# Selective scan of layer 1: the gated input written over u in SBUF, where the state's scan reads it, with four u buffers

## The chip, the cores and the metric

The kernel runs on one core of one Trainium2 chip. The metric is the device time of one launch in microseconds (us). An instruction of one of the engines TensorE (PE in the rows), VectorE (DVE), ScalarE (ACT), GpSimd (POOL) and SyncE (SP, which only issues DMAs here) runs in the order of its engine's program, and the engines wait for each other through semaphores.

## The reference

Two layers over 32 images of 96 channels by 56 x 56 pixels, all in float32. Layer 0 is a depthwise 7x7 convolution, a layer norm over channels, a two-layer MLP and a residual. Layer 1, where the change is, is a depthwise 5x5 convolution with SiLU and then a selective scan over the L = 3136 pixels of an image, with N = 4 states for each channel:

```python
xs = silu(conv5x5(x) + conv_b)                      # (B, D, L)
x_dbl = einsum('kd,bdl->bkl', x_proj_w, xs)         # dts, Bs, Cs
delta = softplus(einsum('dr,brl->bdl', dt_w, dts) + dt_b)
log_dA = maximum(delta[:, :, None] * A, LOG_EPS)
P = exp(cumsum(log_dA, axis=-1))
dB_u = delta[:, :, None] * Bs[:, None] * xs[:, :, None]
hs = P * cumsum(dB_u / maximum(P, EPS), axis=-1)
y = einsum('bdnl,bnl->bdl', hs, Cs) + xs * Ds
```

The kernel computes hs as a recurrence. With d_a = exp(log_dA), q is the running product of d_a that starts at 1/EPS, so that q = P/EPS; the input of the state is multiplied by min(q, 1), which stands for the maximum(P, EPS) of the reference; and h is the recurrence h = d_a * h + min(q, 1) * u.

## The kernel before

The two layers run one after the other. Layer 0 ends near 1,850 us of the profiled execution and layer 1's recurrence runs from 1,988 us to its end.

Layer 1 works on groups of 4 images, so there are 8 groups. 128 partitions hold 32 channels of 4 images, so a group has TILES = 3 such tiles. The 3136 pixels are cut into BANDS = 7 bands of BT = 448. For each band and tile there are N = 4 states, so a band has 12 steps and a group S = 84 steps; the kernel has 672. Every engine's program for a group is a Python loop over the steps s, written out, and its order is the order of the calls; there is no scheduler.

In one step:

- ScalarE writes d_a (L1211 and L1217), five steps ahead, into one of seven buffers.
- GpSimd writes u = dxs * B (`times_b`, L1029), U_AHEAD steps ahead. It multiplies a finished h by C in place (`times_c`, L1042), and, but for the last band, first copies the last column of h (h_last, L1039, a 128x1 addition with zeros). In 3 of 12 steps it also makes dxs = delta * xs (`times_x`, L1017), between the two.
- VectorE runs, for step s: `keep_q` (L1113, a copy of the last column of q, not in the last band), `gate` (L1121), in 3 of 12 steps `sum_delta` (L1095), then `scan_q` of step s + 1 (L1105) and `scan_h` of step s (L1132).
- TensorE adds the four h*C of a tile into ps_y (L1354), and computes the convolution of the next group of images beside it (L1299, L1306, and, in bursts, L1319).

The two q buffers ps_q are PSUM banks. `scan_q` reads d_a from SBUF and a broadcast zero column no_q from PSUM. `gate` reads q and u and writes over q in the PSUM bank. `scan_h` reads d_a from SBUF and the gated values from PSUM, and writes h to SBUF. `sum_delta` reads one operand from PSUM and one from SBUF. GpSimd reads and writes SBUF alone.

GpSimd's program for step s is `times_c` of s - 1, then `times_x` where there is one, then `times_b` of s + U_AHEAD. `times_b` waits until the buffer that it writes is free, which is told by the semaphore gated.

Of the kernel before, what the change touches and what calls it, by code (L numbers as in the profile page):

```python
# [39 lines left out]
BT = BLKS * TOK  # L40
BANDS = L // BT
# [35 lines left out]
SLABS = 3  # L77
AHEAD = 5
ZSTEPS = 3
U_SLOTS = 3  # L80
U_AHEAD = U_SLOTS
H_SLOTS = 6
Y_LAG = 2
Z_SLOTS = 2
DA_SLOTS = 7
# [635 lines left out]
def layer1(nc, groups, x1, t2, consts, out):  # L721
# [4 lines left out]
    with ExitStack() as ctx:  # L726
        def sb(name, shape, dt=F32):
            return ctx.enter_context(nc.sbuf_tensor(name, shape, dt))

        def pb(name):  # L730
            return ctx.enter_context(nc.psum_tensor(name, [128, BANK], F32))

        def sem(name):
            return ctx.enter_context(nc.semaphore(name))
# [22 lines left out]
        d_a = [sb(f"d_a{i}", [128, BT]) for i in range(DA_SLOTS)]  # L757
        b_rows = [sb(f"b_rows{i}", [128, BT]) for i in range(N)]
        u = [sb(f"u{i}", [128, BT]) for i in range(U_SLOTS)]
        c_rows = [sb(f"c_rows{i}", [128, BT]) for i in range(N)]  # L760
        h = [sb(f"h{i}", [128, BT]) for i in range(H_SLOTS)]
# [6 lines left out]
        ps_q = [pb(f"ps_q{i}") for i in range(2)]  # L768
# [25 lines left out]
        gated = sem("gated")  # L794
        h_done = sem("h_done")
        hc_done = sem("hc_done")
        q_kept = sem("q_kept")
# [10 lines left out]
        S = BANDS * STEPS  # L808
        RUNS = BANDS * TILES
        KEPT = (BANDS - 1) * STEPS  # L810
# [73 lines left out]
        def next_band(g, b):  # L884
            return (g, b + 1) if b + 1 < BANDS else (g + 1, 0)
# [114 lines left out]
        @block.gpsimd  # L1000
        def _(pool):
            nc.gpsimd.memset(zeros[:, :], 0.0).then_inc(prepared, 1)
            nc.gpsimd.memset(q_first[:, :], float(np.float32(1) / np.float32(EPS))).then_inc(prepared, 1)
            nc.gpsimd.memset(log_eps[:, 0:1], -LOG_EPS).then_inc(prepared, 1)
            for k in range(Y_SLOTS):
                pool.sem_inc(y_stored[k], 16)
            pool.sem_inc(y_kept, 1)
            pool.sem_inc(h_done, 1)
            pool.sem_inc(gated, 1)
            pool.sem_inc(y_added, H_SLOTS)  # L1010
            pool.wait_ge(prepared, PREPARED)

            def times_x(f, b, t, first=False):
                pool.wait_ge(delta_ready, f * RUNS + b * TILES + t + 1)
                if not first:
                    pool.wait_ge(u_done, (f * BANDS + b - 1) * STEPS + (t + 1) * N)  # L1016
                nc.gpsimd.tensor_tensor(dxs[:, t, :], delta[:, t, :], xs[:, t, b * BT:(b + 1) * BT],  # L1017
                                        ALU.mult).then_inc(dxs_ready, 1)

            def times_b(g, s, first=False):  # L1020

                b, t, n = s // STEPS, s % STEPS // N, s % N
                if t == 0:
                    pool.wait_ge(b_in[n], (g * BANDS + b + 1) * 16)
                if n == 0:
                    pool.wait_ge(dxs_ready, g * RUNS + s // N + 1)
                if not first:
                    pool.wait_ge(gated, g * S + s - U_SLOTS + 2)
                nc.gpsimd.tensor_tensor(u[s % U_SLOTS][:, :], dxs[:, t, :], b_rows[n][:, :],  # L1029
                                        ALU.mult).then_inc(u_done, 1)  # L1030

            def times_c(g, s):

                b, t, n = s // STEPS, s % STEPS // N, s % N
                if t == 0:
                    pool.wait_ge(c_in[n], (g * BANDS + b + 1) * 16)
                pool.wait_ge(h_done, g * S + s + 2)  # L1037
                if b + 1 < BANDS:
                    nc.gpsimd.tensor_tensor(h_last[:, s % STEPS:s % STEPS + 1], h[s % H_SLOTS][:, BT - 1:BT],  # L1039
                                            zeros[:, 0:1], ALU.add).then_inc(h_kept, 1)  # L1040
                    pool.wait_ge(h_kept, g * KEPT + s + 1)
                nc.gpsimd.tensor_tensor(h[s % H_SLOTS][:, :], h[s % H_SLOTS][:, :], c_rows[n][:, :],  # L1042
                                        ALU.mult).then_inc(hc_done, 1)

            def group(g, more, first=False):
                for s in range(S):
                    b, j = s // STEPS, s % STEPS
                    f, fb = next_band(g, b)
                    prepare = more or b + 1 < BANDS

                    if s > 0:
                        times_c(g, s - 1)
                    if prepare and j in DXS_AT:
                        times_x(f, fb, DXS_AT.index(j))
                    if j == DXS_NOW:
                        times_x(g, b, TILES - 1, b == 0 and first)
                    if prepare and j + U_AHEAD == STEPS - N:

                        pool.wait_ge(xd_stored, (f * BANDS + fb + 1) * 16)
                    if s + U_AHEAD < S:  # L1060
                        times_b(g, s + U_AHEAD)
                    elif more:
                        times_b(g + 1, s + U_AHEAD - S)
                times_c(g, S - 1)


            for t in range(TILES - 1):
                times_x(0, 0, t, True)
            for s in range(U_AHEAD):
                times_b(0, s, True)  # L1070
            group(0, True, True)
            with pool.Fori(1, last) as g:
                group(g, True)
            group(last, False)

        @block.vector
        def _(dve):
# [20 lines left out]
            def scan_q(g, s):  # L1098
                b, j = s // STEPS, s % STEPS
                dve.wait_ge(d_a_ready, g * S + s + 1)  # L1100
                dve.wait_ge(h_done, g * S + max(s, 1))
                if s > 1:
                    dve.wait_ge(q_kept, g * KEPT + min(s - 1, KEPT))  # L1103
                first = q_first[:, 0:1] if b == 0 else q_last[:, j:j + 1]
                nc.vector.tensor_tensor_scan(ps_q[s % 2][:, 0:BT], d_a[s % DA_SLOTS][:, :],  # L1105
                                             no_q.broadcast_to([128, BT]), first,
                                             ALU.mult, ALU.add).then_inc(q_done, 1)
# [7 lines left out]
            def gate(g, s):  # L1115
                b = s // STEPS
                dve.wait_ge(q_done, g * S + s + 1)
                if b + 1 < BANDS:
                    dve.wait_ge(q_kept, g * KEPT + s + 1)
                dve.wait_ge(u_done, g * S + s + 1)  # L1120
                nc.vector.scalar_tensor_tensor(ps_q[s % 2][:, 0:BT], ps_q[s % 2][:, 0:BT], 1.0, u[s % U_SLOTS][:, :],  # L1121
                                               ALU.min, ALU.mult).then_inc(gated, 1)

            def scan_h(g, s):
                b, j = s // STEPS, s % STEPS
                dve.wait_ge(gated, g * S + s + 2)
                dve.wait_ge(y_added, g * S + s + 1)
                first = zeros[:, 0:1]
                if b > 0:
                    dve.wait_ge(h_kept, g * KEPT + s - STEPS + 1)  # L1130
                    first = h_last[:, j:j + 1]
                nc.vector.tensor_tensor_scan(h[s % H_SLOTS][:, :], d_a[s % DA_SLOTS][:, :], ps_q[s % 2][:, 0:BT], first,  # L1132
                                             ALU.mult, ALU.add).then_inc(h_done, 1)

            def group(g, more):
                scan_q(g, 0)
                for s in range(S):
                    b, j = s // STEPS, s % STEPS
                    f, fb = next_band(g, b)
                    keep_q(g, s)  # L1140
                    gate(g, s)
                    if (more or b + 1 < BANDS) and j in SUM_AT:
                        sum_delta(f, fb, SUM_AT.index(j))
                    if s + 1 < S:
                        scan_q(g, s + 1)
                    scan_h(g, s)
# [327 lines left out]
```

## Time and profile before

| | |
|---|---|
| median of 3 runs | 4056.53 us (4040.93 to 4058.47) |
| the profiled execution, its own time | 4053.06 us |
| its span, first to last instruction | 4051.3 us |
| a middle group of layer 1, first scan_h to first scan_h of the next | 259.58 us |
| the last group, first to last scan_h | 242.84 us |
| granted TensorE clock, mean | 0.93 |

A span is shorter than the time of its execution by what lies before the first and behind the last instruction, here 1.8 us. Busy times of different engines overlap. An idle time in a row is that of the engine ahead of the instructions of the group, with what ended it behind an arrow.

### The profile page before, as it was taken

The numbers are of one execution on the slowest core, as the hardware profiler recorded it, in microseconds if no ns is written. First come the engines' busy times: TensorE is split into PE (matmuls) and PEld (weight loads), VectorE is DVE, ScalarE is ACT, GpSimd is POOL, SyncE is SP. The second block draws the span as 40 slices with busy tenths as digits, with TensorE's granted clock in tenths as the row PEclk, the third lists the DMA queues.
The fourth block names the chain that finished last, engine by engine and source line by source line (L and its number), as shares of the span: only waits on it lengthen the run. The fifth ranks groups of instructions, "written<-read, shape, count | busy, mean of one in ns | idle before, by whom it ended". The sixth has DMA issues, their size and how long they took to land. (4 is left out here: it accounts for less than half of the span.)

```text
span 4051.3 us, 72657 instructions
## 1 busy us (share of the span) xinstructions
PE 3669.9 (91%) x22358; PEld 2643.2 (65%) x22358; DVE 3170.4 (78%) x4640; ACT 2564.9 (63%) x4292; POOL 2309.4 (57%) x2448
## 2 busy tenths in 40 slices
PE   6999999999999999997899898998989989899776
PEld 6778787979787787867566564664646646556322
DVE  3676858585766768580399899998998989989999
ACT  1453718172645537274688788787877878778764
POOL 0232404141322324140398897988988889888988
PEclk9999999999999999997799898898988989989887
DMA  7546473746465464427565555564546646455321
GB/s 229 166 139 197 103 245 96 248 101 218 120 188 160 133 206 105 169 75 161 137 172 152 146 167 131 168 170 127 169 125 172 181 115 181 133 159 161 94 74 61
DMA packets 383776, 613.07 MB, mean 151 GB/s; under 512 B 199967, under 2 KB 324152, under 8 KB 383048
## 3 DMA queue, kind: packets, MB, share of 16 engines
q1 hardware_dynamic: 383336, 607.74, 52.7%
q8 instruction: 211, 3.46, 0.4%
q14 instruction: 229, 1.88, 0.1%
HBM read 527.35 MB, written 80.28 MB: 150 GB/s over the span
## 5 line engine op out<-in xcount | busy, mean ns | idle before, releaser
L523 ACT ACTIVATE act_h<-ps_up,b 128x448 f32<-128x448 f32 x672 | 408.9, 635 | 781.7 <-PE ps_up L641 781.4
L1354 PE MATMUL ps_y<-h,ident 128*128 128x448 f32 x1344 | 728.8, 630 | 148.3 <-POOL h L1042 118.5
L320 POOL TENSOR_TENSOR h_low<-act_h,h_high 128x448 fp32r<-128x448 f32 x224 | 287.6, 1284 | 901.4 <-ACT h_high L528 901.3
L1042 POOL TENSOR_TENSOR h<-h,c_rows 128x448 f32<-128x448 f32 x672 | 763.8, 1137 | 51.2 <-DVE h L1132 5.6
L1029 POOL TENSOR_TENSOR u<-dxs,b_rows 128x448 f32<-128x448 f32 x672 | 764.4, 1138 | 22.8 <-DVE ps_q L1121 14.7
L1105 DVE TENSOR_TENSOR_SCAN ps_q<-d_a,q_last,ps_q 128x448 f32<-128x448 f32 x576 | 659.7, 1145 | 0.0
L1132 DVE TENSOR_TENSOR_SCAN h<-d_a,h_last,ps_q 128x448 f32<-128x448 f32 x576 | 645.5, 1121 | 0.0
L1306 PEld LDWEIGHTS ps_front<-win,taps 120*112 120x112 f32 x4608 | 538.2, 187 | 148.3 <-issue 146.3
L614 PE MATMUL ps_stage<-win,taps 124*112 124x112 f32 x6144 | 608.0, 260 | 2.7 <-DVE w_low L367 2.7
L614 PEld LDWEIGHTS ps_stage<-win,taps 124*112 124x112 f32 x6144 | 607.8, 178 | 3.3 <-DVE w_low L367 2.8
L1211 ACT ACTIVATE d_a<-delta,log_eps,a_neg 128x448 f32<-128x448 f32 x672 | 503.4, 750 | 119.4 <-DVE h L1132 59.3
L1306 PE MATMUL ps_front<-win,taps 120*112 120x112 f32 x4608 | 541.5, 270 | 5.3 <-ACT win L1168 3.7
L1354 PEld LDWEIGHTS ps_y<-h,ident 128*128 128x128 f32 x1344 | 237.1, 208 | 416.8 <-POOL h L1042 265.1
L315 POOL TENSOR_TENSOR ln_rstd<-ln_var,minus_half 112x7 f32<-112x7 f32 x128 | 244.9, 1913 | 399.8 <-DVE ln_var L402 399.8
L1121 DVE SCALAR_TENSOR_TENSOR ps_q<-ps_q,u 128x448 f32<-128x448 f32 x672 | 422.4, 629 | 54.6 <-POOL u L1029 31.0
L430 DVE TENSOR_TENSOR conv<-ps_stage,bias_row 112x448 f32<-112x448 f32 x192 | 180.4, 940 | 349.9 <-PE ps_stage L614 349.9
L1217 ACT ACTIVATE d_a<-d_a 128x448 f32<-128x448 f32 x672 | 387.6, 577 | 8.3
L1168 ACT ACTIVATE conv<-ps_front 112x448 f32<-112x448 f32 x192 | 181.8, 947 | 208.5 <-PE ps_front L1306 208.5
L1299 PEld LDWEIGHTS ps_front<-ident,x1pad 32*120 32x120 f32 x2880 | 202.1, 146 | 147.3 <-issue 145.8
L637 PE MATMUL ps_up<-hn_high,w_high 96*128 96x448 f32 x672 | 253.7, 378 | 34.7 <-DVE hn_low L412 19.9
L1017 POOL TENSOR_TENSOR dxs<-delta,xs 128x448 f32<-128x448 f32 x168 | 191.1, 1138 | 140.1 <-DVE delta L1095 140.1
L1168 ACT ACTIVATE win<-ps_front 120x480 f32<-120x480 f32 x192 | 203.5, 1061 | 91.5 <-PE ps_front L1299 89.1
(82 smaller groups left out, 6267.3 us busy)
## 6 DMA issues: line engine op xcount, KB each, us to landing
taps<-in_t_dram SPq DMA_DIRECT2D x192, 896.0 KB, 5.1
taps<-in_t_dram SPq DMA_DIRECT2D x192, 672.0 KB, 4.6
b_rows<-bc_dram SPq DMA_DIRECT2D x224, 224.0 KB, 2.9
c_rows<-bc_dram SPq DMA_DIRECT2D x224, 224.0 KB, 3.1
xres<-in_x_dram SPq DMA_DIRECT2D x224, 168.0 KB, 2.5
x_dram<-x1o SPq DMA_DIRECT2D x224, 168.0 KB, 2.0
x1pad<-x_dram SPq DMA_DIRECT2D x96, 392.0 KB, 5.7
out_dram<-y SPq DMA_DIRECT2D x168, 224.0 KB, 2.7
```

What stands on the lines that cost most here:

```text
L523: nc.scalar.activation(act_h[u % 2][:, t, :], ps_up[t][:, 0:BT], ACT.Gelu, bias=b1[:, t:t + 1]).then_inc(gelu_done, 1)
L614: mm = nc.tensor.matmul(ps_stage[q % 2][0:TOK, c * BLOCKS:(c + 1) * BLOCKS], taps[q % SLOTS1][0:WIN1, c, k, :], win[:, q * CQ + c, :, k:k ...
L1029: nc.gpsimd.tensor_tensor(u[s % U_SLOTS][:, :], dxs[:, t, :], b_rows[n][:, :], ALU.mult).then_inc(u_done, 1)
L1042: nc.gpsimd.tensor_tensor(h[s % H_SLOTS][:, :], h[s % H_SLOTS][:, :], c_rows[n][:, :], ALU.mult).then_inc(hc_done, 1)
L1105: nc.vector.tensor_tensor_scan(ps_q[s % 2][:, 0:BT], d_a[s % DA_SLOTS][:, :], no_q.broadcast_to([128, BT]), first, ALU.mult, ALU.add).then ...
L1121: nc.vector.scalar_tensor_tensor(ps_q[s % 2][:, 0:BT], ps_q[s % 2][:, 0:BT], 1.0, u[s % U_SLOTS][:, :], ALU.min, ALU.mult).then_inc(gated, 1)
L1132: nc.vector.tensor_tensor_scan(h[s % H_SLOTS][:, :], d_a[s % DA_SLOTS][:, :], ps_q[s % 2][:, 0:BT], first, ALU.mult, ALU.add).then_inc(h_d ...
L1168: nc.scalar.activation(dst, src, ACT.Copy).then_inc(front_kept, 1)
L1211: nc.scalar.activation(d_a[s % DA_SLOTS][:, :], delta[:, t, :], ACT.Relu, bias=log_eps[:, 0:1], scale=a_neg[:, t, n:n + 1]).then_inc(clipp ...
L1217: nc.scalar.activation(d_a[s % DA_SLOTS][:, :], d_a[s % DA_SLOTS][:, :], ACT.Exp, bias=LOG_EPS).then_inc(d_a_ready, 1)
L1306: mm = nc.tensor.matmul(bank[i][0:TOK, c * BLOCKS:(c + 1) * BLOCKS], taps[n % SLOTS2][0:WIN2, c, w, :], win[cb % 2][:, k * CQ + c, :, w:w ...
L1354: nc.tensor.matmul(total, ident[:, :], h[s % H_SLOTS][:, :], start=False, stop=(n == N - 1)).then_inc(y_added, 1)
```

## The change

`gate` now writes its result over u in SBUF, and `scan_h` reads it there. Since q in the PSUM bank isn't overwritten any more, `gate` doesn't wait for the copy of q's last column (q_kept), and `scan_q` waits for a gate (gated) in place of a scan (h_done). Since u now lives until `scan_h` has read it, there are four u buffers for three, with the same lead U_AHEAD = 3, and `times_b` waits for h_done in place of gated. No instruction of computation or DMA is added, removed or moved.

```diff
--- before.py
+++ after.py
@@ -77,8 +77,8 @@
 SLABS = 3
 AHEAD = 5
 ZSTEPS = 3
-U_SLOTS = 3
-U_AHEAD = U_SLOTS
+U_SLOTS = 4
+U_AHEAD = U_SLOTS - 1
 H_SLOTS = 6
 Y_LAG = 2
 Z_SLOTS = 2
@@ -1025,7 +1025,7 @@
                 if n == 0:
                     pool.wait_ge(dxs_ready, g * RUNS + s // N + 1)
                 if not first:
-                    pool.wait_ge(gated, g * S + s - U_SLOTS + 2)
+                    pool.wait_ge(h_done, g * S + s - U_SLOTS + 2)
                 nc.gpsimd.tensor_tensor(u[s % U_SLOTS][:, :], dxs[:, t, :], b_rows[n][:, :],
                                         ALU.mult).then_inc(u_done, 1)
 
@@ -1098,7 +1098,7 @@
             def scan_q(g, s):
                 b, j = s // STEPS, s % STEPS
                 dve.wait_ge(d_a_ready, g * S + s + 1)
-                dve.wait_ge(h_done, g * S + max(s, 1))
+                dve.wait_ge(gated, g * S + max(s, 1))
                 if s > 1:
                     dve.wait_ge(q_kept, g * KEPT + min(s - 1, KEPT))
                 first = q_first[:, 0:1] if b == 0 else q_last[:, j:j + 1]
@@ -1115,10 +1115,8 @@
             def gate(g, s):
                 b = s // STEPS
                 dve.wait_ge(q_done, g * S + s + 1)
-                if b + 1 < BANDS:
-                    dve.wait_ge(q_kept, g * KEPT + s + 1)
                 dve.wait_ge(u_done, g * S + s + 1)
-                nc.vector.scalar_tensor_tensor(ps_q[s % 2][:, 0:BT], ps_q[s % 2][:, 0:BT], 1.0, u[s % U_SLOTS][:, :],
+                nc.vector.scalar_tensor_tensor(u[s % U_SLOTS][:, :], ps_q[s % 2][:, 0:BT], 1.0, u[s % U_SLOTS][:, :],
                                                ALU.min, ALU.mult).then_inc(gated, 1)
 
             def scan_h(g, s):
@@ -1129,7 +1127,7 @@
                 if b > 0:
                     dve.wait_ge(h_kept, g * KEPT + s - STEPS + 1)
                     first = h_last[:, j:j + 1]
-                nc.vector.tensor_tensor_scan(h[s % H_SLOTS][:, :], d_a[s % DA_SLOTS][:, :], ps_q[s % 2][:, 0:BT], first,
+                nc.vector.tensor_tensor_scan(h[s % H_SLOTS][:, :], d_a[s % DA_SLOTS][:, :], u[s % U_SLOTS][:, :], first,
                                              ALU.mult, ALU.add).then_inc(h_done, 1)
 
             def group(g, more):
```

VectorE's instructions at the start of a group of images, before. The names are buffers without their numbers, a waited semaphore stands in brackets, this view prints both scans as SCALAR_TENSOR_TENSOR, and an ISA or REGISTER_ALU row is no computation:

```order
L1105 SCALAR_TENSOR_TENSOR ps_q<-d_a,q_first,ps_q 128x448 [waits h_done,d_a_ready]
L1113 COPY q_last<-ps_q 128x1 [waits q_done]
L1119 ISA [waits q_done]
L1121 SCALAR_TENSOR_TENSOR ps_q<-ps_q,u 128x448 [waits u_done,q_kept]
L1100 REGISTER_ALU
L1105 SCALAR_TENSOR_TENSOR ps_q<-d_a,q_first,ps_q 128x448 [waits h_done,d_a_ready]
L1132 SCALAR_TENSOR_TENSOR h<-d_a,zeros,ps_q 128x448 [waits y_added,gated]
```

And the same place of the changed kernel:

```order
L1105 SCALAR_TENSOR_TENSOR ps_q<-d_a,q_first,ps_q 128x448 [waits gated,d_a_ready]
L1113 COPY q_last<-ps_q 128x1 [waits q_done]
L1119 SCALAR_TENSOR_TENSOR u<-ps_q,u 128x448 [waits u_done,q_done]
L1100 REGISTER_ALU
L1105 SCALAR_TENSOR_TENSOR ps_q<-d_a,q_first,ps_q 128x448 [waits gated,d_a_ready]
L1130 SCALAR_TENSOR_TENSOR h<-d_a,zeros,u 128x448 [waits y_added,gated]
```

The order of the computing instructions is the same. The gate writes u, the state's scan reads d_a and u, and the gate's separate wait is gone.

## Rows read from the trace of the kernel before

**Rows 1.** The page: span, then busy time and share of each engine.

```profile
span 4051.3 us, 72657 instructions
PE 3669.9 (91%) x22358; PEld 2643.2 (65%) x22358; DVE 3170.4 (78%) x4640; ACT 2564.9 (63%) x4292; POOL 2309.4 (57%) x2448
```

**Rows 2.** Windows by group: PE, PEld, DVE, ACT, POOL busy, clock, DMA.

```profile
2765.26:3024.84 259.58, 237.97 (x1314) 146.41 (x1314) 242.55 (x346) 206.51 (x337) 222.20 (x262) 0.91 0.56 153
...
3801.69:4044.53 242.84, 172.91 (x291) 54.79 (x290) 236.35 (x339) 145.39 (x244) 214.45 (x255) 0.78 0.23 69
```

**Rows 3.** Groups of VectorE, 2765.26 to 3024.84 us: busy, mean ns, idle before.

```profile
L1132 DVE TENSOR_TENSOR_SCAN h<-d_a,h_last,ps_q 128x448 f32<-128x448 f32 x72 | 80.7, 1121 | 0.0
L1121 DVE SCALAR_TENSOR_TENSOR ps_q<-ps_q,u 128x448 f32<-128x448 f32 x84 | 52.8, 629 | 7.7 <-POOL u L1029 5.2
L1095 DVE SCALAR_TENSOR_TENSOR delta<-ps_prep,z_log 128x448 f32<-128x448 f32 x21 | 13.0, 617 | 7.4 <-ACT z_log L1193 7.4
L1113 DVE COPY q_last<-ps_q 128x1 f32<-128x1 f32 x72 | 9.5, 132 | 0.0
```

**Rows 4.** The same view of GpSimd, same window.

```profile
L1029 POOL TENSOR_TENSOR u<-dxs,b_rows 128x448 f32<-128x448 f32 x85 | 96.9, 1140 | 3.6 <-DVE ps_q L1121 3.5
L1017 POOL TENSOR_TENSOR dxs<-delta,xs 128x448 f32<-128x448 f32 x21 | 23.9, 1139 | 0.0
L1039 POOL TENSOR_TENSOR h_last<-h,zeros 128x1 f32<-128x1 f32 x72 | 13.8, 192 | 29.7 <-DMA c_rows<-bc_dram 19.5 <-DVE h L1132 9.6
```

**Rows 5.** Timeline of VectorE: start us, us, engine, line, operation.

```profile
2914.41 1.12 DVE L1132 TENSOR_TENSOR_SCAN h<-d_a,h_last,ps_q 128x448 f32<-128x448 f32 x1
2915.45 0.13 DVE L1113 COPY q_last<-ps_q 128x1 f32<-128x1 f32 x1
2915.61 0.63 DVE L1121 SCALAR_TENSOR_TENSOR ps_q<-ps_q,u 128x448 f32<-128x448 f32 x1
2916.16 1.15 DVE L1105 TENSOR_TENSOR_SCAN ps_q<-d_a,q_last,ps_q 128x448 f32<-128x448 f32 x1
2917.21 1.12 DVE L1132 TENSOR_TENSOR_SCAN h<-d_a,h_last,ps_q 128x448 f32<-128x448 f32 x1
```

**Rows 6.** Timeline of GpSimd beside it.

```profile
2914.41 1.14 POOL L1029 TENSOR_TENSOR u<-dxs,b_rows 128x448 f32<-128x448 f32 x1
2915.61 0.19 POOL L1039 TENSOR_TENSOR h_last<-h,zeros 128x1 f32<-128x1 f32 x1
2915.88 1.14 POOL L1042 TENSOR_TENSOR h<-h,c_rows 128x448 f32<-128x448 f32 x1
2916.98 1.13 POOL L1029 TENSOR_TENSOR u<-dxs,b_rows 128x448 f32<-128x448 f32 x1
2918.47 0.19 POOL L1039 TENSOR_TENSOR h_last<-h,zeros 128x1 f32<-128x1 f32 x1 [0.36 <-DVE h L1132]
```

**Rows 7.** Layer 0, single lines: duration in ns, least/median/most.

```profile
L395 DVE TENSOR_TENSOR conv<-conv,ln_mean x128: 835/844/857, 138.3 to 1812.8; 112x672 f32<-112x672 f32 x128
L406 DVE TENSOR_TENSOR conv<-conv,ln_rstd x128: 833/1222/1816, 142.7 to 1819.3; 112x672 f32<-112x672 f32 x128
L412 DVE TENSOR_TENSOR hn_low<-ps_back,hn_high x224: 607/615/623, 145.3 to 1827.1; 96x448 fp32r<-96x448 f32 x112
L424 DVE TENSOR_TENSOR h_low<-act_h,h_high x224: 607/618/985, 154.7 to 1832.7; 128x448 fp32r<-128x448 f32 x112
L320 POOL TENSOR_TENSOR h_low<-act_h,h_high x224: 1126/1157/2128, 153.1 to 1831.8; 128x448 fp32r<-128x448 f32 x112
```

**Rows 8.** Timelines of layer 0, VectorE and GpSimd, near 168 us.

```profile
167.12 2.12 POOL L320 TENSOR_TENSOR h_low<-act_h,h_high 128x448 fp32r<-128x448 f32 x1 [0.34 <-ACT h_high L528]
167.40 0.83 DVE L406 TENSOR_TENSOR conv<-conv,ln_rstd 112x672 f32<-112x672 f32 x1
```

**Rows 9.** The same two timelines near 183 us.

```profile
182.62 1.14 POOL L320 TENSOR_TENSOR h_low<-act_h,h_high 128x448 fp32r<-128x448 f32 x1
182.68 1.80 DVE L406 TENSOR_TENSOR conv<-conv,ln_rstd 112x672 f32<-112x672 f32 x1
```

## The prediction

> **What bounds the kernel now.** I read the page's busy times first [rows 1]. PE is busy 91% of the span, but that is a mean over two layers, and the change touches only the recurrence of layer 1, so I cut that into its groups of 84 steps. A middle group takes 259.58 us [rows 2]: PE is busy for 238, VectorE for 242.55 and GpSimd for 222.20. Then I looked at who waits for what. The two scans and the copy of VectorE never wait, its gate waits 7.7 us and its delta 7.4 us in a whole group [rows 3]. The timeline shows the same from near: from one scan_h to the next VectorE takes 2917.21 - 2914.41 = 2.80 us without a hole, in the order copy, gate, scan_q, scan_h [rows 5]. So VectorE sets the pace. GpSimd is nearly as full: in the same step it runs h_last, h*C and u, and has 0.36 us left before the next h [rows 6]. The last group, in which no convolution of a next group runs beside, takes 242.84 us [rows 2]. Against 259 for the others that puts some 16 us a group on waits around the bursts of TensorE and ScalarE. The reader should keep two things: two engines are nearly full, and they work side by side.
>
> **What the change does, part by part.** No instruction is added or removed, and each engine keeps its order. Four things differ.
>
> 1. The gate's result goes to SBUF. sum_delta is an instruction of the same form (one PSUM, one SBUF operand, SBUF output) and takes 617 ns against the gate's 629 [rows 3]. That saves 0.012 us x 672 = 8 us, if VectorE still sets the pace.
>
> 2. The gate doesn't wait for the copy of q. Before, the copy starts 2915.45, which is 0.08 us before the scan ahead of it ends, and the gate starts 2915.61, 0.03 us after the copy ends [rows 5]. If the gate too may start 0.08 us before the end of the one ahead, that is 0.11 us a step, in 72 of 84 steps: 576 x 0.11 = 63 us. Bounds: nothing, and those 63 us, under the same condition.
>
> 3. Four u buffers with the wait for h_done. times_b(s + 3) now needs the scan_h of s - 1, and times_c(s - 1), which stands ahead of it on GpSimd, has waited for that already. So this wait costs nothing, and the old one, 3.5 us a group [rows 4], is gone. A u is still made three steps ahead. scan_q's new wait is for a gate two steps back, which stands ahead of it on VectorE: nothing.
>
> 4. scan_h reads d_a and the gated input from SBUF, where one of the two came from PSUM. This is where I put the result. In layer 1 before, no VectorE instruction beside GpSimd has two SBUF inputs, and scan_h takes 1121 ns in the mean although GpSimd nearly always runs [rows 3, 5, 6]. In layer 0 there are such instructions. L395 and L406 have the same shape and two SBUF inputs each. L395 takes 835 to 857 ns, L406 takes 833 to 1816 [rows 7], and the timeline says why: where GpSimd's L320 is 0.06 us ahead (182.62), L406 takes 1.80 us instead of 0.84 and ends 0.72 us after L320 does [rows 9]. Where L406 has come first, it takes 0.83 us, and L320 takes 2.12 instead of 1.16 and ends 169.24, 1.01 us after L406's end at 168.23 [rows 8]. L412, with one PSUM input, is never longer than 623 ns [rows 7]. So a VectorE instruction with two SBUF inputs and a GpSimd instruction that reads SBUF run one after the other, and what is hidden of the second is only its start: 0.84 - 0.72 = 0.12 us on VectorE. The Trainium skill, "SBUF — State Buffer", section "Who interferes with whom", states this as a rule: a VectorE instruction with two SBUF inputs contends with a GpSimd one that reads SBUF, and the second to issue fully blocks. The trace agrees, by these same rows.
>
> All of GpSimd's instructions in the recurrence read SBUF, so each scan_h has to stand apart from all of them. A scan after a block is 1.12 - 0.12 = 1.00 us.
>
> **The new step, order A.** GpSimd waits for h, then runs h*C and u. From the end of a scan_h at 2918.33: h_last starts 0.14 later, the product 0.27 after that (2915.88 - 2915.61), u 1.10 after that, and u takes 1.13: 2.64 us [rows 5, 6]. VectorE would issue its next scan_h 1.68 us after the end of the last (2917.21 - 2915.53), or 2.2 with a delta between, so it finds GpSimd in u, and waits to its end. Step: 2.64 + 1.00 = 3.64 us.
>
> **Order B.** The scan gets in between the product and u. Then u ends 1.01 us after the scan, h_last starts some 0.06 later, the product 0.27 after that, and takes 1.14: 2.48, and with the scan 3.48 us. Nothing in the trace shows who wins when VectorE has been waiting and GpSimd has its next instruction ready, so I take the middle and keep both ends.
>
> A step without h_last is 0.27 shorter (12 of 84), and each dxs adds 1.10 (21 in a group [rows 4]). Group by A: 72 x 3.64 + 12 x 3.37 + 21 x 1.10 = 325.6 us. By B: 72 x 3.48 + 12 x 3.21 + 23.1 = 312.2. Middle 319. The savings of points 1 and 2 are on VectorE, which now waits for GpSimd anyway, so they count nothing. The 16 us of waits in a group were waits for work of TensorE and ScalarE and for c_rows (19.5 us [rows 4]), which a longer step hides in part; I keep 5, with 0 and 16 as ends. TensorE's 238 us fit into 319 even at the last group's clock of 0.78 instead of 0.91 (278 us), and ScalarE's 206 do.
>
> **Sum.** Before, from the first scan_h to the last: 7 x 259 + 243 = 2056 us. After: 8 x 319 + 7 x 5 = 2587. That is 531 more on the profiled execution's 4053: 4584 us, and this execution lies 3 us under the median of the runs, so 4585. Ends: B without waits 8 x 312.2 = 2498, +442, 4495 us; A with all of them 2605 + 112 = 2717, +661, 4714 us.
>
> A second rule would speak for the change: "VectorE: DVE Perf Modes" of the Trainium skill gives, in its section on the trn2 errata, a fixed cost of 120 cycles for a PSUM source and 58 for an SBUF source. By it, scan_h would save 62 cycles at 0.96 GHz, 0.065 us, or an estimated 43 us over 672 steps. The trace doesn't agree: L412 (PSUM and SBUF) has a median of 615 ns and L424 (both SBUF) of 618 [rows 7]. The sum goes by the trace.
>
> **The rivals.**
>
> - The scan shares instead of excluding: it takes nearly twice as long as an elementwise instruction of its length (1121 ns for 448 elements, L424 618 [rows 3, 7]), so it may read only half of the time, and GpSimd in the gaps. If half of the 1.00 us is lost, 0.50 less GpSimd's slack against VectorE, (242.55 - 222.20) / 84 = 0.24 us a step, is 0.26 x 672 = 175 us: 4230 us. Against it: in rows 8 and 9 the wait is whole. Chance 0.06.
> - Other side, faster: a tensor_tensor_scan, of which no row shows two SBUF inputs, doesn't block at all. Then points 1 to 3 hold: 8 + 63 and up to 3.5 x 7 = 25 us of u's waits, 4057 less 71 to 96, near 3975 us. GpSimd's 222 us a group would still fit. It decides whether L1130 stays at 1.12 us beside a GpSimd that runs. Against it: layer 0's blocked instructions differ in nothing but the operation. Chance 0.05.
> - Points 1 and 2 don't pay either, because something else is the pace, and nothing blocks: 4050 us. Chance 0.02.
> - Worse than A: while VectorE waits, a gate or a late c_rows makes both engines wait in turn, 4 us a step or more: above 4720 us. Chance 0.07.
>
> **How the numbers follow.** Full exclusion between the ends of A and B has 0.80, and its own range is 4495 to 4714. The rivals below it are too small and too far away to be taken in; I widen the low end a little for a start that is hidden on both sides: 4450 to 4715. A change under 0.5% (20 us) can't be told from none. Slower: 0.80 + 0.06 + 0.07 = 0.93; same 0.02; faster 0.05.
>
> **What would show it.** L1130 should be longer than 1.12 us nearly always, with a mean near 2 in A (issued 1.68 us after the scan before, ended after 3.64) and near 1.8 in B, where L1029 is near 2 too. Distances between scan_h should be 3.5 to 3.7 us, 4.6 to 4.8 with dxs, and a group 312 to 342 us. Layer 0 shouldn't change. L1119 should take 617 ns. I am wrong if scan_h stays at 1.12 us and GpSimd at 1.14, or if a group's length is made by idle time before L1039 or L1119 that isn't a block.

## The result and the profile after

The changed kernel takes 4387.58 us (median of 4 runs, 4379.04 to 4396.49) against 4057.5 us for the kernel before (median of 4 runs beside it), a ratio of 1.0814 with a 95% interval of 1.0786 to 1.0842. That is slower, as forecast, but by 330 us and not by the 531 of the sum; it lies under the low end of 4450. In what follows a block is the time for which an instruction of one engine is held because one of the other engine runs, and a hand-over is the time from the end of the one to the end or the start of the next.

The page, span and busy times of the engines:

```profile
span 4385.5 us, 72645 instructions
PE 3821.2 (87%) x22358; PEld 2700.4 (62%) x22358; DVE 3426.1 (78%) x4640; ACT 2576.0 (59%) x4292; POOL 2801.8 (64%) x2448
```

GpSimd's busy time rose from 2309.4 us to 2801.8 and VectorE's from 3170.4 to 3426.1 [rows 1], with the same instructions. The first scan_h starts at 1994.45 us, where it was 1988.50. That is no change of layer 0: in the profiled executions of all runs of this document, whose layer 0 is the same, it starts between 1980 and 1999 us.

The windows by group, cut at the first scan_h of each (columns as in [rows 2]), a middle one and the last:

```profile
2589.67:2892.48 302.81, 260.64 (x1315) 156.03 (x1314) 273.17 (x346) 208.53 (x336) 282.99 (x262) 0.85 0.49 131
...
4092.73:4376.70 283.97, 194.59 (x290) 61.31 (x290) 266.16 (x338) 143.50 (x244) 278.32 (x256) 0.67 0.20 58
```

A middle group takes 302.81 us where it took 259.58, the last 283.97 where it took 242.84. From the first scan_h to the last, 2382 us where it was 2056: 326 of the 334 us between the spans. TensorE isn't what made the groups longer: the middle group grew by 43 us with PE busy for 260.64 of 302.81 us at a granted clock of 0.85 (0.91 before), and the last one grew by 41 with PE busy for 194.59 of 283.97.

The groups of VectorE in that middle window (busy, mean ns, idle before), to set against [rows 3]:

```profile
L1130 DVE TENSOR_TENSOR_SCAN h<-d_a,h_last,u 128x448 f32<-128x448 f32 x72 | 113.0, 1570 | 0.0
L1119 DVE SCALAR_TENSOR_TENSOR u<-ps_q,u 128x448 f32<-128x448 f32 x84 | 51.1, 608 | 14.7 <-POOL u L1029 14.7
L1095 DVE SCALAR_TENSOR_TENSOR delta<-ps_prep,z_log 128x448 f32<-128x448 f32 x21 | 12.8, 612 | 10.9 <-ACT z_log L1191 10.9
```

And those of GpSimd, against [rows 4]:

```profile
L1029 POOL TENSOR_TENSOR u<-dxs,b_rows 128x448 f32<-128x448 f32 x85 | 116.9, 1375 | 0.8 <-DMA bc_dram<-xd 0.8
L1017 POOL TENSOR_TENSOR dxs<-delta,xs 128x448 f32<-128x448 f32 x21 | 28.6, 1360 | 0.0
L1039 POOL TENSOR_TENSOR h_last<-h,zeros 128x1 f32<-128x1 f32 x72 | 47.4, 658 | 13.4 <-DMA c_rows<-bc_dram 11.0 <-DVE h L1130 2.4
L1042 POOL TENSOR_TENSOR h<-h,c_rows 128x448 f32<-128x448 f32 x84 | 99.3, 1182 | 5.6
```

scan_h has a mean of 1570 ns for 1121. On the other engine u has 1375 for 1140, dxs 1360 for 1139 and h_last 658 for 192; the product L1042 has 1182. GpSimd's idle time ahead of these shrank: h_last waits 2.4 us for scan_h where it was 9.6. So the time is in longer instructions of both engines. Over the whole run, durations least/median/most:

```profile
L1130 DVE TENSOR_TENSOR_SCAN h<-d_a,h_last,u x576: 1123/1680/2055, 2037.5 to 4376.7; 128x448 f32<-128x448 f32 x192
L1130 DVE TENSOR_TENSOR_SCAN h<-d_a,zeros,u x96: 1118/1670/2061, 1994.4 to 4129.0; 128x448 f32<-128x448 f32 x96
L1119 DVE SCALAR_TENSOR_TENSOR u<-ps_q,u x672: 591/608/626, 1992.9 to 4376.1; 128x448 f32<-128x448 f32 x168
L1039 POOL TENSOR_TENSOR h_last<-h,zeros x576: 179/969/1052, 1995.7 to 4347.1; 128x1 f32<-128x1 f32 x192
```

scan_h takes at least 1118 to 1123 ns: reading SBUF in place of PSUM made it no faster by itself, and no slower either. The trace holds the comparison: 15 of the 672 scan_h are issued while GpSimd runs nothing, and they take 1123 to 1126 ns. The other 657 are issued while a GpSimd instruction runs, and every one of them ends 0.94 us or more after that instruction does. h_last, a 128x1 addition, has a median of 969 ns, five times its length alone.

The timeline of VectorE in one step:

```profile
2998.94 1.68 DVE L1130 TENSOR_TENSOR_SCAN h<-d_a,h_last,u 128x448 f32<-128x448 f32 x1
3000.54 0.12 DVE L1113 COPY q_last<-ps_q 128x1 f32<-128x1 f32 x1
3000.59 0.61 DVE L1119 SCALAR_TENSOR_TENSOR u<-ps_q,u 128x448 f32<-128x448 f32 x1
3001.12 1.14 DVE L1105 TENSOR_TENSOR_SCAN ps_q<-d_a,q_last,ps_q 128x448 f32<-128x448 f32 x1
3002.18 1.69 DVE L1130 TENSOR_TENSOR_SCAN h<-d_a,h_last,u 128x448 f32<-128x448 f32 x1
```

and that of GpSimd beside it:

```profile
3000.68 1.14 POOL L1042 TENSOR_TENSOR h<-h,c_rows 128x448 f32<-128x448 f32 x1
3001.77 1.14 POOL L1029 TENSOR_TENSOR u<-dxs,b_rows 128x448 f32<-128x448 f32 x1
3002.87 0.98 POOL L1039 TENSOR_TENSOR h_last<-h,zeros 128x1 f32<-128x1 f32 x1
3003.93 1.13 POOL L1042 TENSOR_TENSOR h<-h,c_rows 128x448 f32<-128x448 f32 x1
```

This is the commonest step of the new kernel, 3002.18 - 2998.94 = 3.24 us. scan_h is issued at 3002.18, while u runs on GpSimd (3001.77 to 2.91), and ends at 3003.87, 0.96 after u does. h_last is issued at 3002.87 as u ends, but the scan that has been waiting goes first, and h_last ends with it. The product follows at 3003.93. So the scan and GpSimd's instructions stand one behind the other, as forecast. What the forecast didn't have is the place: between u and h_last. And GpSimd is a step behind: this h_last was issued before the running scan ended, so it takes the h of the scan before.

The forecast's order B occurs too. The scan of VectorE first, then GpSimd:

```profile
2000.72 1.68 DVE L1130 TENSOR_TENSOR_SCAN h<-d_a,zeros,u 128x448 f32<-128x448 f32 x1
```

```profile
2000.31 1.13 POOL L1042 TENSOR_TENSOR h<-h,c_rows 128x448 f32<-128x448 f32 x1
2001.41 1.92 POOL L1029 TENSOR_TENSOR u<-dxs,b_rows 128x448 f32<-128x448 f32 x1
2003.30 0.18 POOL L1039 TENSOR_TENSOR h_last<-h,zeros 128x1 f32<-128x1 f32 x1
2003.56 1.14 POOL L1042 TENSOR_TENSOR h<-h,c_rows 128x448 f32<-128x448 f32 x1
```

Here u is the instruction that is held, and from product to product it is 2003.56 - 2000.31 = 3.25 us, the same. Counted from product to product over steps with h_last and without dxs, 300 hold h_last and 71 hold u, both with a median of 3.24 us.

### The profile page after: what moved, and what is told of

The parts are those of the page before. It is cut to its first block and busy times, and to the rows that moved or that the text cites. A ratio compares the mean times of both kernels' runs of the same rounds, so it can differ in the third digit from the quotient of the medians.

```text
span 4385.5 us, 72645 instructions
## 1 busy us (share of the span) xinstructions
PE 3821.2 (87%) x22358; PEld 2700.4 (62%) x22358; DVE 3426.1 (78%) x4640; ACT 2576.0 (59%) x4292; POOL 2801.8 (64%) x2448
## 5 line engine op out<-in xcount | busy, mean ns | idle before, releaser
L1352 PE MATMUL ps_y<-h,ident 128*128 128x448 f32 x1344 | 797.9, 683 | 357.8 <-POOL h L1042 347.6
L1029 POOL TENSOR_TENSOR u<-dxs,b_rows 128x448 f32<-128x448 f32 x672 | 936.8, 1394 | 2.9 <-DMA bc_dram<-xd 2.7
L1130 DVE TENSOR_TENSOR_SCAN h<-d_a,h_last,u 128x448 f32<-128x448 f32 x576 | 904.4, 1570 | 0.0
L1042 POOL TENSOR_TENSOR h<-h,c_rows 128x448 f32<-128x448 f32 x672 | 802.3, 1194 | 45.2
L1304 PEld LDWEIGHTS ps_front<-win,taps 120*112 120x112 f32 x4608 | 553.9, 192 | 152.6 <-issue 150.1
L1304 PE MATMUL ps_front<-win,taps 120*112 120x112 f32 x4608 | 556.6, 275 | 6.0 <-ACT win L1166 3.7
L1119 DVE SCALAR_TENSOR_TENSOR u<-ps_q,u 128x448 f32<-128x448 f32 x672 | 409.0, 609 | 123.6 <-POOL u L1029 123.6
L1039 POOL TENSOR_TENSOR h_last<-h,zeros 128x1 f32<-128x1 f32 x576 | 374.4, 650 | 76.0 <-DMA c_rows<-bc_dram 63.3
L1017 POOL TENSOR_TENSOR dxs<-delta,xs 128x448 f32<-128x448 f32 x168 | 219.7, 1308 | 138.3 <-DVE delta L1095 138.3
```

Of the source, the lines that this page charges most:

```text
L1119: nc.vector.scalar_tensor_tensor(u[s % U_SLOTS][:, :], ps_q[s % 2][:, 0:BT], 1.0, u[s % U_SLOTS][:, :], ALU.min, ALU.mult).then_inc(gated, 1)
L1304: mm = nc.tensor.matmul(bank[i][0:TOK, c * BLOCKS:(c + 1) * BLOCKS], taps[n % SLOTS2][0:WIN2, c, w, :], win[cb % 2][:, k * CQ + c, :, w:w ...
L1352: nc.tensor.matmul(total, ident[:, :], h[s % H_SLOTS][:, :], start=False, stop=(n == N - 1)).then_inc(y_added, 1)
```

## Experiments

The kernel before ran beside the others in each of three sessions, with medians of 4064.13 us (experiments 1 to 4), 4053.54 (5, 6, 8, 9) and 4058.46 (7, 10, 11). Each ratio is to the one of its session.

**1. Four u buffers alone.** Is it the buffers and their wait?

```diff
-U_SLOTS = 3
-U_AHEAD = U_SLOTS
+U_SLOTS = 4
+U_AHEAD = U_SLOTS - 1
-                    pool.wait_ge(gated, g * S + s - U_SLOTS + 2)
+                    pool.wait_ge(h_done, g * S + s - U_SLOTS + 2)
```

> The kernel before with four u buffers and times_b waiting for h_done, the gate still in PSUM: point 3 of the prediction alone. Theory of exclusion (two SBUF inputs of the state's scan against GpSimd's reads): nothing is blocked, 4030 to 4057 us, the state's scan at 1.12 us. Rival (the u buffers or the new wait cost the time): near the changed kernel's 4388 us.

4056.95 us against 4064.13, ratio 0.9986 (0.9968 to 1.0004), as expected. The buffers and the wait cost nothing, and gain nothing that can be measured.

**2. The changed kernel, but the scan reads PSUM.** What is left without point 4?

```diff
-                dve.wait_ge(gated, g * S + max(s, 1))
+                dve.wait_ge(h_done, g * S + max(s, 1))
-                nc.vector.tensor_tensor_scan(h[...], d_a[...], u[s % U_SLOTS][:, :], first,
+                nc.vector.tensor_tensor_scan(h[...], d_a[...], ps_q[s % 2][:, 0:BT], first,
```

> The changed kernel, but the state's scan reads q in PSUM as it stands and not the gated input, so the product with min(q, 1) is left out of h; the gate still runs and writes over u in SBUF, without a wait for the copy of q. Points 1, 2 and 3 without point 4. Theory of exclusion: the state's scan has one SBUF input again, takes 1.12 us, and the step is shorter by the 0.11 us of the gate's wait: 3975 to 3995 us. Rival (the gate's write to SBUF beside GpSimd costs the time): near 4388 us. If 4050 us, the gate's wait was worth nothing.

4016.8 us against 4064.13, ratio 0.9883 (0.986 to 0.9905): a gain, but a smaller one than the 3975 to 3995 us expected. The product with min(q, 1) is left out of h here, so h is not the layer's h; every instruction still runs, scan_h with a median of 1121 ns. The gate still writes to SBUF over u, so neither is the cost; the second SBUF operand of the scan alone is. Its VectorE timeline:

```profile
2916.52 1.12 DVE L1130 TENSOR_TENSOR_SCAN h<-d_a,h_last,ps_q 128x448 f32<-128x448 f32 x1
2917.55 0.13 DVE L1113 COPY q_last<-ps_q 128x1 f32<-128x1 f32 x1
2917.60 0.61 DVE L1119 SCALAR_TENSOR_TENSOR u<-ps_q,u 128x448 f32<-128x448 f32 x1
2918.14 1.15 DVE L1105 TENSOR_TENSOR_SCAN ps_q<-d_a,q_last,ps_q 128x448 f32<-128x448 f32 x1
2919.19 1.12 DVE L1130 TENSOR_TENSOR_SCAN h<-d_a,h_last,ps_q 128x448 f32<-128x448 f32 x1
```

The gate starts 0.05 us after the copy starts, where it was 0.16 [rows 5], and the step is 2.67 us where it was 2.80. That is the 0.11 us of point 2, and a little for the gate itself. But 0.13 x 576 = 75 us were to be expected from the steps that have the copy, and the kernel gained 47 on its median. The last group fell from 242.8 to 229.7 us; the groups before it take 252 to 260 us where they took 257 to 261.

**3. The kernel before with one operand moved.** Is it bound to this change at all?

```diff
-                                             no_q.broadcast_to([128, BT]), first,
+                                             zeros[:, 0:1].broadcast_to([128, BT]), first,
```

> The kernel before with one operand moved: the q scan reads its constant zero from an SBUF column in place of a PSUM column. No buffer, wait or order differs. Theory of exclusion: now the q scan, 1.145 us, has two SBUF inputs and each costs GpSimd and VectorE as the state's scan does in the changed kernel: 4370 to 4450 us. If it is bound to the gated input, the u buffers or the write to SBUF: 4057 us. If the broadcast of a single column takes no reads after the first: 4057 us too.

4391.03 us against 4064.13, ratio 1.0815 (1.0786 to 1.0845), inside the 4370 to 4450 us of the theory and the same as the changed kernel's. The two scans on VectorE:

```profile
L1105 DVE TENSOR_TENSOR_SCAN ps_q<-d_a,q_last,zeros 128x448 f32<-128x448 f32 x576 | 868.6, 1508 | 0.0
L1132 DVE TENSOR_TENSOR_SCAN h<-d_a,h_last,ps_q 128x448 f32<-128x448 f32 x576 | 643.5, 1117 | 0.0
```

and u on GpSimd:

```profile
L1029 POOL TENSOR_TENSOR u<-dxs,b_rows 128x448 f32<-128x448 f32 x672 | 1083.6, 1613 | 10.0 <-DMA bc_dram<-xd 6.5 <-DVE ps_q L1121 3.5
```

Now the q scan is the long one, 1508 ns for 1145, and scan_h is back at 1117. One operand in SBUF instead of PSUM does it, in either scan, even where it is a single column read 448 times.

**4. Both scans with two SBUF operands.** The same edit in the changed kernel.

> The changed kernel with the q scan's zero in SBUF too, so both scans have two SBUF inputs. Theory of exclusion: a second block in each step costs as much as the first, some 0.78 us x 672 = 520 us: 4800 to 4950 us. Rival (what is lost is a fixed toll of this kernel's order, or VectorE's slack takes the second block): under 4500 us.

4873.76 us, ratio 1.1994 (1.1963 to 1.2026), inside the 4800 to 4950 us expected. The second block costs 486 us over the changed kernel, 0.72 us a step. The first cost 4388 - 4017 = 371 against run 2, 0.55 us a step. It is likely less because VectorE and not GpSimd set the pace there; no run separates this. Both scans are long:

```profile
L1130 DVE TENSOR_TENSOR_SCAN h<-d_a,h_last,u 128x448 f32<-128x448 f32 x576 | 1118.8, 1942 | 0.0
L1105 DVE TENSOR_TENSOR_SCAN ps_q<-d_a,q_last,zeros 128x448 f32<-128x448 f32 x576 | 877.2, 1523 | 0.0
```

**5 and 6. The lead of u.** Why 3.24 us and not 3.48 to 3.64? The changed kernel with three buffers (a lead of two steps) and with two (a lead of one):

```diff
-U_SLOTS = 4
+U_SLOTS = 3   # and 2
 U_AHEAD = U_SLOTS - 1
```

> The changed kernel with u made two steps ahead in place of three (three buffers). Question: why was the step 3.24 us and not the 3.48 to 3.64 forecast? Theory (GpSimd runs one step behind VectorE, so that the h it wants is finished before the block and h_last is issued under the scan that blocks it): a lag of one step needs a lead of two, so nothing changes: 4380 to 4420 us. Rival (the short step needs the full lead of three, since VectorE must be two steps ahead): above 4500 us.

> The changed kernel with u made one step ahead (two buffers). Now a gate needs the u that GpSimd makes right after the product before, so GpSimd can't run a step behind: order A of the prediction is forced. From the rows of the changed kernel a blocked scan ends 0.97 us after GpSimd's instruction, so the step is 0.14 + 0.27 + 1.10 + 1.13 + 0.97 = 3.61 us, 0.37 over 3.24, x 672 = 249: 4600 to 4650 us, and h_last near its unblocked 0.19 us. Rival (the forecast was too high because each hand-over is shorter, whatever the order): 4400 to 4450 us.

With a lead of two 4380.59 us, ratio 1.0801 (1.0774 to 1.0828): nothing changes, as the first theory has it. h_last is still the blocked one:

```profile
L1039 POOL TENSOR_TENSOR h_last<-h,zeros x576: 181/971/992, 1993.5 to 4340.4; 128x1 f32<-128x1 f32 x192
```

With a lead of one 4533.05 us, ratio 1.118 (1.1152 to 1.1208). It is 145 us more than the changed kernel, so the order matters, but 4600 to 4650 was a miss. The timeline of VectorE's scan and the next one:

```profile
3002.61 1.96 DVE L1130 TENSOR_TENSOR_SCAN h<-d_a,h_last,u 128x448 f32<-128x448 f32 x1
3006.12 1.98 DVE L1130 TENSOR_TENSOR_SCAN h<-d_a,h_last,u 128x448 f32<-128x448 f32 x1
```

and of GpSimd:

```profile
3002.48 1.13 POOL L1029 TENSOR_TENSOR u<-dxs,b_rows 128x448 f32<-128x448 f32 x1
3004.64 0.19 POOL L1039 TENSOR_TENSOR h_last<-h,zeros 128x1 f32<-128x1 f32 x1 [1.03 <-DVE h L1130]
3004.91 1.14 POOL L1042 TENSOR_TENSOR h<-h,c_rows 128x448 f32<-128x448 f32 x1
...
3021.18 1.91 POOL L1029 TENSOR_TENSOR u<-dxs,b_rows 128x448 f32<-128x448 f32 x1
```

This is order A of the prediction. The scan ends at 3004.57, 0.96 after u, and h_last starts 0.07 later, at its own 0.19 us. The step is 3.51 us (3006.12 - 3002.61). GpSimd now waits for h, in total us, times and longest:

```profile
POOL h_last L1039 <- DVE h L1130: 436.4, 410, 5.7
```

0.14 us from the scan's end to h_last was too much by 0.07. And steps with dxs take 4.33 us from product to product, not 3.61 + 1.10 = 4.71: there the scan gets in between dxs and u, and u, issued at 3021.18 and 1.91 us long, hides its start behind it.

**7. The copy of h's last column on VectorE.** Does it matter what stands behind the block? In the changed kernel:

```diff
-                    nc.gpsimd.tensor_tensor(h_last[...], h[s % H_SLOTS][:, BT - 1:BT],
-                                            zeros[:, 0:1], ALU.add).then_inc(h_kept, 1)
+                    nc.vector.tensor_tensor(h_last[...], h[s % H_SLOTS][:, BT - 1:BT],
+                                            no_q, ALU.add).then_inc(h_kept, 1)
```

On VectorE the copy for step s - 1 stands behind the copy of q of step s; the rest of the edit (GpSimd's wait for it, the call) is left out above.

> The changed kernel with the copy of h's last column on VectorE (one SBUF, one PSUM operand) in place of GpSimd. In the changed kernel h_last is issued under the scan that blocks it. Theory (a block costs 0.78 us whatever stands behind it, since either instruction hides its own start there; the last band, which has no h_last, shows steps of 2.97 against 3.24 us): 576 x 0.27 = 155 us less than the changed kernel, 4215 to 4260 us. Rival (h_last is hidden by the scan and costs only the 0.06 us behind it): 4340 to 4365 us.

4283.66 us, ratio 1.0567 (1.0525 to 1.0608): 104 less than the changed kernel, between the theory's 4215 to 4260 us and the rival's 4340 to 4365. GpSimd's timeline:

```profile
3013.88 1.12 POOL L1040 TENSOR_TENSOR h<-h,c_rows 128x448 f32<-128x448 f32 x1
3014.97 1.92 POOL L1029 TENSOR_TENSOR u<-dxs,b_rows 128x448 f32<-128x448 f32 x1
3016.85 1.13 POOL L1040 TENSOR_TENSOR h<-h,c_rows 128x448 f32<-128x448 f32 x1
```

The step is 3016.85 - 13.88 = 2.97 us, so the first theory has its step right and its total too low, and u is the blocked instruction (1.92 us for 1.14). The rest of the 155 us is likely in a new wait of GpSimd for the copy on VectorE, which no run takes away:

```profile
POOL h L1040 <- DVE h_last L1116: 114.9, 83, 4.6
```

**8. The copy of q's last column on ScalarE.** A try for a faster kernel from the kernel before.

```diff
-                    nc.vector.tensor_copy(q_last[:, j:j + 1], ps_q[s % 2][:, BT - 1:BT]).then_inc(q_kept, 1)
+                    nc.scalar.activation(q_last[:, j:j + 1], ps_q[s % 2][:, BT - 1:BT], ACT.Copy).then_inc(q_kept, 1)
```

> The kernel before, with the copy of q's last column on ScalarE in place of VectorE; the gate and both scans keep one PSUM operand each. A step of VectorE falls from 2.80 to 2.61 us (as in the last band, where there is no copy). Theory (what the middle groups can gain is limited by waits for TensorE and ScalarE, as they stayed at 259 us when the step fell by 0.13 us): only the last group and the start gain, 14 us and a few: 4020 to 4050 us. Rival (VectorE sets the pace everywhere): 576 x 0.19 = 109 us less: 3950 us. Rival (ScalarE comes late with the copy and the gate waits): above 4057 us.

4109.75 us, ratio 1.0136 (1.0114 to 1.0157), slower by 1.4%: the third case, and not the 4020 to 4050 us of the theory. The copy stands first in ScalarE's step. The gate's waits for it, in total us, times and longest:

```profile
DVE ps_q L1115 <- ACT q_last L1154: 229.8, 196, 6.7
```

**9. The same with four u buffers.**

> The same with the four u buffers and their wait for h_done, which takes GpSimd's waits for a gate away. Theory: within 10 us of the run without them. Rival (the waits of u for a gate limit the run without them): 20 us or more below it.

4105.52 us, ratio 1.0115 (1.0091 to 1.014), within the 10 us expected and not to be told from 8.

**10. The gate shifted by a column.** Point 2 can be had in PSUM, if q's last column is out of the gate's way:

```diff
-                nc.vector.tensor_tensor_scan(ps_q[s % 2][:, 0:BT], d_a[...],
+                nc.vector.tensor_tensor_scan(ps_q[s % 2][:, 1:BT + 1], d_a[...],
-                if b + 1 < BANDS:
-                    dve.wait_ge(q_kept, g * KEPT + s + 1)
-                nc.vector.scalar_tensor_tensor(ps_q[s % 2][:, 0:BT], ps_q[s % 2][:, 0:BT], 1.0, u[...],
+                nc.vector.scalar_tensor_tensor(ps_q[s % 2][:, 0:BT], ps_q[s % 2][:, 1:BT + 1], 1.0, u[...],
```

Left out above: the copy reads column BT, and the zero column no_q moves one column on.

> The kernel before, but q stands one column to the right in its PSUM bank (columns 1 to 448) and the gate writes its result to columns 0 to 447, so the last column of q survives and the gate needn't wait for its copy. Every VectorE instruction keeps one PSUM operand, three u buffers. Theory (the gate's wait is worth what the run with the gate in SBUF and the scan on q showed, 1.2%, and nothing blocks): 4005 to 4025 us against a kernel before of 4055. Rival (that gain came from the gate's SBUF output or the u buffers): 4057 us.

4013.68 us against 4058.46, ratio 0.9899 (0.9869 to 0.9929), inside the 4005 to 4025 us expected. It is faster than both kernels: it has the change's gain and not its cost. The scan keeps its length, and the gate is at 617 ns where it was 629, though it still writes to PSUM:

```profile
L1130 DVE TENSOR_TENSOR_SCAN h<-d_a,h_last,ps_q 128x448 f32<-128x448 f32 x576 | 644.0, 1118 | 0.0
L1119 DVE SCALAR_TENSOR_TENSOR ps_q<-ps_q,u 128x448 f32<-128x448 f32 x672 | 414.5, 617 | 39.9 <-POOL u L1029 39.9
```

**11. The same with four u buffers.**

> The same with four u buffers and the wait for h_done. Theory: within 8 us of the run without them, as the four u buffers alone gave 0.14% with an interval that holds nothing. Rival (the waits for a gate matter once VectorE is faster): 10 us or more below it.

4025.6 us, ratio 0.991 (0.9883 to 0.9938): 12 us above run 10 where 8 were allowed for, but the intervals overlap nearly whole, so three buffers do.

## Why the prediction was wrong in its size

- **Point 4, exclusion: right, and shown.** Experiments 1 and 2 take the buffers, the waits and the gate's SBUF output out of it, and 3 brings the whole loss into the kernel before with one operand. "SBUF — State Buffer" of the Trainium skill, section "Who interferes with whom", says that a VectorE instruction with two SBUF inputs contends with a GpSimd one that reads SBUF, and not with one that only writes it; here it holds for tensor_tensor_scan, 1.12 us while GpSimd runs nothing and 1.57 in the mean in a middle group. That it is GpSimd's reading and not its writing is the page's word: every GpSimd instruction here does both. The rivals "shares" (4230 us) and "doesn't block" (3975 us) fall.
- **The new step: the step that failed.** The sum took the middle of "2.64 + 1.00 = 3.64 us" (order A) and "3.48 us" (order B); the kernel's step is 3.24. Of the 205 us by which 2587 lies over the 2382 measured from the first scan_h to the last, 151 are B's own size: with 5 us of waits a group B alone gives 8 x 312.2 + 35 = 2533. The other 54 are the half of the way to A, which hardly occurs. The distances between scan_h that it named as a sign, 3.5 to 3.7 us, came out at 3.24, and the mean of scan_h, near 1.8 to 2 us, at 1.57.
- **The hand-overs.** They came from layer 0 (1.01 us for GpSimd behind a block, 0.12 us of VectorE's start hidden) and from a single row (0.14 us from a scan to h_last). B's sum was 1.01 + 0.06 + 0.27 + 1.14 + 1.00. The order B step shown above has 0.93 from the scan's end to u's end, h_last 0.03 before that end and not 0.06 behind it, 0.26, 1.13, and 0.96 for the scan behind the product: 3.25 us. A was too high as well: run 6 forces it and measures 0.07 us to h_last, 0.96 for the scan behind u, 3.51 us for the step and 4.33 for a step with dxs where the sum had 4.74. From the first scan_h to the last that run takes 2530 us where A with 5 us of waits a group was 8 x 325.6 + 35 = 2640.
- **The order.** A has GpSimd waiting for h. In the changed kernel it hardly does (12.7 us in the whole run, against 436.4 in run 6): GpSimd is a step behind and finds h finished, and a scan that has waited gets in before its next instruction, whichever that is. That the blocks themselves bring GpSimd to this lag is my reading, which no run shows. The prediction left open who goes first and gave A half the weight. The place is mostly before h_last, which B didn't have, and at times between product and u, as B has it; both give 3.24 us. Runs 5 and 6 show that the short step takes a lead of two steps and is worth 145 us against a lead of one.
- **Savings of points 1 and 2: right that they count nothing here.** Run 2 shows that they exist without point 4: the gate has a median of 614 ns where it was 632, and starts 0.11 us earlier. But the reason of point 1 is not borne out. Run 10 has a mean of 617 ns with the output still in PSUM, so most of what the gate saves doesn't come from its output. And the rival that carried these savings, 71 to 96 us, was too hopeful: 47 us was measured. In the middle groups the faster step is mostly used up by waits. What these groups wait for wasn't tested.
- **Point 3: right.** Run 1.
- **Waits.** 5 us a group were kept. Steps of 3.24, 2.97 in the last band and 1.09 for a dxs give 72 x 3.24 + 12 x 2.97 + 21 x 1.09 = 292 us, and a middle group takes 299 to 303: some 9.
- **A slip in the sum.** The execution with 4053 us lies 3 us under the median, which makes 4584 into 4587 and not 4585, and the ends 4495 and 4714 go without the 3 us. It doesn't bear on the account.
- **The rule on PSUM sources.** "VectorE: DVE Perf Modes" of the Trainium skill gives an SBUF source a smaller fixed cost. scan_h takes at least 1118 to 1123 ns from SBUF in the changed kernel, and at least 1118 to 1119 from PSUM in the kernel before: no gain, as the prediction read it from layer 0.

## What to carry to other kernels

Count the SBUF inputs of each VectorE instruction that runs beside GpSimd: one operand in PSUM, even a constant column, keeps the two engines apart here, and moving it cost the kernel 330 us for the first scan of 1.12 us (0.49 a step) and 486 for the second (0.72 a step). When two engines exclude each other, the price isn't the length of the instruction but that less the starts that it hides, and with enough buffers the one that is held back can run a step behind: take the hand-over times from rows of the same stage, in both orders, and look for the order in which nobody waits twice. If a wait is the only thing to be gained, look for a way round it that leaves the operands where they are (here one column to the right).

## What the runs showed of the hardware that wasn't expected

- A 128x1 instruction of GpSimd is held by the same time as a large one: h_last takes 969 ns for 191, u 1.92 us for 1.14.
- When VectorE's scan waits while GpSimd works and GpSimd has its next instruction ready, the scan goes first: scan at 3002.18 and h_last at 3002.87 in the timeline of the changed kernel, and in all 526 such places of its trace. There the scan had waited at least 0.32 us. In run 3 it is so in 527 places, with 0.29 us of waiting or more; in 7 others the scan had waited 0.10 us or less, and there GpSimd's instruction went first.
- An operand that is one column broadcast over 448 elements counts as an SBUF input like any other (run 3: 1508 ns for 1145). The second input of L406 in layer 0 is a broadcast too, so the trace of before already hinted at it.
- Behind a block a scan ends 0.96 us after GpSimd's instruction (0.95 in the median of the changed kernel), 0.16 less than its 1.12. A GpSimd instruction of 1.14 us ends 0.92 to 0.94 us behind the scan in the changed kernel, and 1.00 to 1.02 behind L406 in layer 0.
